# A kernel's opening on five queues: reordered, with a shorter statistics chain and more filler products

## The chip, the cores and the metric

The kernel runs on one core of a Trainium2 chip. The metric is the device time of one launch in microseconds (us). Engines are named as the profile names them: PE (TensorE products), PEld (its weight loads), DVE (VectorE), ACT (ScalarE), POOL (GpSimd) and SP (SyncE, which here issues most DMAs).

## The reference

Two layers on x of shape (2, 1024, 2048), with a context of (2, 2048, 2048).

```python
def fake_quant(x, scale, zp):
    q = jnp.clip(jnp.round(x / scale + zp), 0.0, 255.0)
    return (q - zp) * scale

# layer 1: the normalized x and the context are both quantized to bytes
x = x + jnp.matmul(fake_quant(_layernorm(x), s1, z1), fake_quant(ctx, s2, z2))

# layer 2: a base product with bias, and a two-of-eight mixture of rank-16 products
xf = _layernorm(x)
base = xf @ W_base.T + b_base
probs = jax.nn.softmax(xf @ W_router.T)          # top 2 kept, renormalized -> w
lora = einsum('ter,eor,te->to', einsum('td,erd->ter', xf, lora_A), lora_B, w) * 2.0
x = x + base + lora
```

`_layernorm` is (x - mean) / sqrt(var + 1e-5) over the last axis.

## The kernel before

**Tiles.** The rows of x are 16 row tiles T of 128 rows, eight for each half b of the batch. The first product is made for 32 column tiles n (16 for each b); each has three chunks c of 342 columns of rows. `chunk(n, c)` is 16 products, 128x128 by 128x342, into one of four PSUM banks in turn (`RING`); it needs its ring slot read by `take_y` four chunks earlier in `ORDER`, and the bytes of three, six or eight row tiles (`NEED`). The first three n run chunk by chunk across n: (0,0), (1,0), (2,0), (0,1) and so on; from n = 3 the three chunks of one n follow each other.

**A row tile's path.** DVE takes statistics of the 2048 elements in four instructions and aggregates them (`ln_stats_of`, lines 926 and 929), copies the mean and adds epsilon to the variance (936, 937). ACT takes the root (`ln_std_of`, 692). DVE makes scale and shift with a reciprocal and one Newton step (`ln_scale_of`, 944 to 955): seven small instructions, of which each but one waits for the one before. Some tiles go through this in pairs (`LN_GROUPS`: rows 0, 1, 2 alone, then 3+4, 5+6, 7 alone, then pairs). ACT makes the bytes (`ln_bytes_of`, 701), or for rows 4 and 6 POOL (`row_bytes_of`, 1628). PE turns the bytes (`turn`, 1669, eight transposes), ACT copies them out of PSUM as f16 (`ln_copy`, 709), and PE sums them (`row_sum`, 1677).

**A column tile's path.** SP loads 1 MB of context, POOL makes bytes (`ctx_bytes_of`, 1614), and ACT (`ctx_act_of`, 718, for n in `ON_ACT`) or DVE (`ctx_ready_of`, 988, the others) makes f16. DVE takes each chunk's result (`take_y`, 1003). When the third chunk of n is taken, ACT adds a column, writes the high part and squares (724, 732, 740), and DVE writes the low part and adds up the squares (`lo_of` 1009, `acc_of` 1022). `load_xt(n)` on SP waits for these of n - 3.

**The order around the change.** Each engine's queue is written out by hand. PE's opening is lines 1720 to 1748: row tiles 0 to 2, 16 filler products of ones (`keep_busy`, 1716, a result that nobody reads), then chunks (0,0) and (1,0), and after that turns, row sums and chunks mixed. DVE's opening is lines 1045 to 1153, ACT's 742 to 791, SP's 470 to 498. `LOAD_AT`, `STATS_AT`, `SCALE_AT`, `STD_AT` and `BYTES_AT` say at which n a row tile of the second half is loaded, measured, scaled and made into bytes. `rows[1]` has two slots, so row tile 11 loads only when the bytes of row tile 9 are made; POOL makes the bytes of rows 4 and 6 behind the context bytes of n = 2 and 3 (`POOL_AT`).

Of the kernel before, what the change touches and what calls it, by code (L numbers as in the profile page):

```python
# [8 lines left out]
ALU = mybir.AluOpType  # L9
# [3 lines left out]
P = 128  # L13
# [14 lines left out]
TT = TOKENS // P  # L28
# [29 lines left out]
POOL_AT = {2: 4, 3: 6}  # L58
LOAD_AT = {4: 11, 6: 12, 8: 13, 10: 14, 12: 15}
# [3 lines left out]
ON_ACT = list(range(2, STEPS, 2))  # L63
# [29 lines left out]
def xattn_ffn(nc, x, xT, ctx, s1, z1, s2, z2, w_t, w_n, bias, ar, b_t, outT):  # L93

    es = ExitStack()
    with es:
# [94 lines left out]
        lnt = [small(f"lnt{s}", [P, 8, 2]) for s in range(2)]  # L191
        par = small("par", [P, 25])
# [24 lines left out]
        def pc(i):  # L217
            return par[:, i:i + 1]
# [5 lines left out]
        T0, T1, T2, NIS1 = pc(21), pc(22), pc(23), pc(24)  # L224
# [12 lines left out]
        def sem(name):  # L237
            return es.enter_context(nc.semaphore(name))
# [38 lines left out]
        ln_shift = sem("ln_shift")  # L277
# [165 lines left out]
        def _(sp):  # L443
# [237 lines left out]
        def _(act):  # L681
# [6 lines left out]
            def ln_std_of(g):  # L688

                t0, w = LN_GROUPS[g]  # L690
                act.wait_ge(ln_var, g + 1)
                A.activation(std1[:, t0:t0 + w], lnt[g % 2][:, 0, 0:w], ACT.Sqrt).then_inc(ln_std, 1)
# [59 lines left out]
            ln_std_of(3)  # L752
            ln_bytes_of(3)
            ctx_act_of(2)
# [11 lines left out]
            ctx_act_of(4)  # L766

            for n in range(STEPS):
                col_add_of(n)
                if n == JT + 13:  # L770
                    act.wait_ge(ar_lo, 1)
                hi_of(n)
                if n in STD_AT:
                    ln_std_of(STD_AT[n])
                sq_of(n)
                if n == 0:
                    ln_copy(TT)
                if n == 1:
                    ln_bytes_of(TT + 1)
                if n + 3 in ON_ACT and n + 3 > 4:  # L780
                    ctx_act_of(n + 3)
                if n == 2:
                    ln_copy(TT + 1)
                if n in BYTES_AT:
                    ln_bytes_of(BYTES_AT[n])
                if n - 1 in BYTES_AT:
                    ln_copy(BYTES_AT[n - 1])
                if n == JT + 11:
                    act.wait_ge(ar_scaled, 1)
                    A.activation(ar_p[0][:, :, 0:AR], ar_f[:, :, :], ACT.Copy, scale=asc[:, 0:1]).then_inc(ar_hi, 1)  # L790
# [123 lines left out]
        def _(dve):  # L914
            V = nc.vector

            def ln_stats_of(T):
# [19 lines left out]
                V.tensor_scalar(lnt[g % 2][:, 0, 0:w], mv[g % 2][:, 0:w, 1], EPS, None, ALU.add).then_inc(ln_var, 1)  # L937

            def ln_scale_of(g):

                t0, w = LN_GROUPS[g]
                n = lnt[g % 2]
                dve.wait_ge(ln_std, g + 1)
                V.reciprocal(n[:, 1, 0:w], std1[:, t0:t0 + w]).then_inc(ln_newton, 1)
                dve.wait_ge(ln_newton, 4 * g + 1)
                V.scalar_tensor_tensor(n[:, 2, 0:w], n[:, 1, 0:w], -0.5, n[:, 1, 0:w], ALU.mult, ALU.mult).then_inc(ln_newton, 1)
                dve.wait_ge(ln_newton, 4 * g + 2)
                V.tensor_tensor(n[:, 2, 0:w], n[:, 2, 0:w], n[:, 0, 0:w], ALU.mult).then_inc(ln_newton, 1)
                dve.wait_ge(ln_newton, 4 * g + 3)
                V.scalar_tensor_tensor(n[:, 3, 0:w], n[:, 2, 0:w], 1.5, n[:, 1, 0:w], ALU.add, ALU.mult).then_inc(ln_newton, 1)  # L950
                dve.wait_ge(ln_newton, 4 * g + 4)
                V.tensor_scalar(n[:, 4, 0:w], n[:, 3, 0:w], IS1, None, ALU.mult)
                V.scalar_tensor_tensor(n[:, 6, 0:w], n[:, 3, 0:w], NIS1, mv[g % 2][:, 0:w, 0], ALU.mult, ALU.mult).then_inc(ln_shift, 1)
                dve.wait_ge(ln_shift, g + 1)
                V.tensor_scalar(n[:, 5, 0:w], n[:, 6, 0:w], Z1, None, ALU.add).then_inc(ln_scale, 1)
# [67 lines left out]

            V.memset(onesF[:, :], 1.0)
# [12 lines left out]
            ins.then_inc(ln_stat, 1)  # L1037
            dve.wait_ge(par_turned, 1)
# [6 lines left out]
            ln_stats_of(0)  # L1045
            dve.wait_ge(par_step, 1)
            V.tensor_scalar(NIS1, IS1, -1.0, None, ALU.mult)
# [16 lines left out]
            ctx_ready_of(1)  # L1064
# [32 lines left out]
            bound(0)  # L1097

# [551 lines left out]
        def _(pe):  # L1650
# [301 lines left out]
```

## Time and profile before

| | us |
|---|---|
| median of 3 runs | 1002.93 (1002.04 to 1003.18) |
| the profiled execution's own time | 1003.91 |
| its span, first to last instruction | 1002.1 |
| mean granted TensorE clock | 0.991 of full |

The profile's page gives busy time by engine, the chain of work that ended last, and the costliest groups. The timeline gives instructions of one engine in order of time, merged where the same line repeats; the idle time in front of each stands in square brackets, with what ended it. The windows give each engine's busy time in a stretch, with the granted clock (1.00 is 2.4 GHz, 0.50 is 1.2 GHz). After about 95 us the kernel is the rest of the first product, then the router and rank-16 products, and from about 345 us the large base products.

### The profile page before, as it was taken

Reading aid. Unit: us, or ns where it says so; the run is one execution under the profiler, and the core shown is the slowest. Engines: PE = TensorE matmul, PEld = TensorE weight load, DVE = VectorE, ACT = ScalarE, POOL = GpSimd, SP = SyncE. Lnnn points to the kernel's source line nnn. Section 1 sums busy time; section 2 is a strip of 40 time slices with the busy share of each in tenths; the row PEclk is TensorE's granted clock in tenths of the full one; section 3 lists DMA queues with packets and bytes.
Section 4 is the critical chain, followed back from the end, with each engine's and each line's share of the span. In section 5 each row is a group of like instructions: output and inputs, shape, how many; then the busy total and the mean of one; then the engine's idle time right before and its main releaser. Section 6 shows DMA issues by size and latency. Waiting matters only on the chain.

```text
span 1002.1 us, 14914 instructions
## 1 busy us (share of the span) xinstructions
PE 964.9 (96%) x5765; PEld 523.2 (52%) x5765; DVE 794.9 (79%) x1457; ACT 430.5 (43%) x467; POOL 136.7 (14%) x176
## 2 busy tenths in 40 slices
PE   1798999999999999999999999999999999999998
PEld 1565666666689644444444444444444444444444
DVE  7977877989746677997887777857789788798885
ACT  4667879565643335545443344212222223322310
POOL 3615335456200000000000000000000000000000
PEclk9799999999999999999999999999999999999999
DMA  9837767788542517876765564248544143242220
GB/s 372 362 106 300 263 278 286 250 302 299 202 161 74 153 51 220 249 271 188 227 226 201 174 217 149 79 155 291 185 142 136 59 152 116 79 137 91 98 74 32
DMA packets 62311, 185.65 MB, mean 185 GB/s; under 512 B 6896, under 2 KB 19488, under 8 KB 56096
## 3 DMA queue, kind: packets, MB, share of 16 engines
q1 hardware_dynamic: 58648, 174.18, 48.7%
q0 software_dynamic: 1280, 2.12, 2.4%
q10 hardware_dynamic: 2312, 8.39, 2.1%
q8 instruction: 46, 0.75, 0.3%
q14 instruction: 25, 0.20, 0.1%
HBM read 151.07 MB, written 33.60 MB: 184 GB/s over the span
## 4 chain that ended last, share of the span: by engine, by line
PE 85%; DVE 0%; issue 0%
PE pair L1846 33%; PE pair L1870 28%; PE pair L1689 13%; PE pair L1808 5%; PE pair L1818 4%; PE pair L1882 1%; PE pair L1697 0%; PE pair L1788 0%; PE pair L1669 0%; PE pair L1709 0%; DVE sq L1541 0%; DVE u L1543 0%; PE pair L1703 0%; PE pair L1795 0%; PE pair L1782 0%; PE pair L1713 0%
## 5 line engine op out<-in xcount | busy, mean ns | idle before, releaser
L1846 PE MATMUL pair<-x2p,w_p 128*128 128x512 f16 x1536 | 337.0, 379 | 0.0
L1846 PEld LDWEIGHTS pair<-x2p,w_p 128*128 128x128 f16 x1536 | 150.2, 98 | 180.5
L1689 PE MATMUL pair<-q1T,ctx_q 128*128 128x342 f16 x1536 | 232.6, 313 | 6.3 <-DVE xt L1003 6.3
L1689 PEld LDWEIGHTS pair<-q1T,ctx_q 128*128 128x128 f16 x1536 | 149.6, 98 | 84.7 <-issue 8.2
L1870 PE MATMUL pair<-x2p,w_slot 128*128 128x512 f16 x744 | 163.8, 379 | 0.0
L827 ACT ACTIVATE sq<-pair,lsc 128x512 f32<-128x512 f32 x64 | 43.5, 681 | 212.2 <-PE pair L1818 176.4
L1614 POOL TENSOR_SCALAR ctx_u<-ctx_f,par 128x512 uint8<-128x512 f32 x128 | 112.0, 889 | 142.1 <-DMA ctx_f<-in_ctx 104.0
L1870 PEld LDWEIGHTS pair<-x2p,w_slot 128*128 128x128 f16 x744 | 72.7, 98 | 87.9
L855 ACT ACTIVATE w_slot<-w_q,usc 128x1024 f16<-128x1024 f32 x32 | 36.5, 1146 | 89.8 <-DVE usc L1447 27.2
L1870 PE MATMUL pair<-x2p,x2p 128*128 128x512 f16 x336 | 74.3, 379 | 0.0
L724 ACT ACTIVATE xt<-xt,colt 128x1024 f32<-128x1024 f32 x32 | 36.7, 1146 | 53.9 <-DVE xt L1003 53.9
L1009 DVE SCALAR_TENSOR_TENSOR x2p<-xt,xs,x2p 128x1024 f16<-128x1024 f32 x32 | 42.3, 1322 | 21.1 <-ACT x2p L732 20.9
L1471 DVE SCALAR_TENSOR_TENSOR w_slot<-w_q,usc,w_slot 128x1024 f16<-128x1024 f32 x32 | 40.6, 1282 | 22.8 <-ACT w_slot L855 22.8
L811 ACT ACTIVATE w_p<-w_f,wsc 128x1024 f16<-128x1024 f32 x32 | 34.9, 1138 | 50.1 <-DVE wsc L1216 50.1
L855 ACT ACTIVATE x2p<-w_q,usc 128x1024 f16<-128x1024 f32 x24 | 27.4, 1146 | 65.6 <-DVE usc L1447 15.8
L1003 DVE SCALAR_TENSOR_TENSOR xt<-pair,par,xt 128x342 f32<-128x342 f32 (+1 forms) x96 | 53.5, 564 | 2.5 <-PE pair L1689 2.3
L1870 PEld LDWEIGHTS pair<-x2p,x2p 128*128 128x128 f16 x336 | 32.9, 98 | 39.6
L1870 PE MATMUL pair<-x2p 128*128 128x512 f16 x240 | 52.9, 379 | 0.0
L1818 PE MATMUL pair<-hwT,b_p 128*128 128x512 f16 x192 | 51.7, 379 | 0.0
L1416 DVE SCALAR_TENSOR_TENSOR u<-sq,bias_s,u 128x512 f32<-128x512 f32 x63 | 47.4, 752 | 2.2
L1808 PE MATMUL pair<-ar_p,x2p 128*128 128x137 f16 x768 | 48.3, 224 | 0.0
L1808 PEld LDWEIGHTS pair<-ar_p,x2p 128*128 128x128 f16 x768 | 48.1, 98 | 0.1
(223 smaller groups left out, 1068.0 us busy)
## 6 DMA issues: line engine op xcount, KB each, us to landing
ctx_f<-in_ctx SPq DMA_DIRECT2D x32, 1024.0 KB, 7.6
xt<-in_xT SPq DMA_DIRECT2D x32, 512.0 KB, 4.5
w_r<-in_w_n SPq DMA_DIRECT2D x32, 512.0 KB, 6.9
w_f<-in_w_t SPq DMA_DIRECT2D x32, 512.0 KB, 5.6
w_q<-in_w_t SPq DMA_DIRECT2D x32, 512.0 KB, 5.1
outT<-u SPq DMA_DIRECT2D x63, 256.0 KB, 3.2
rows<-in_x SPq DMA_DIRECT2D x15, 1024.0 KB, 9.4
x_kept<-xt ACTq DMA_DIRECT2D x16, 512.0 KB, 4.3
```

Source lines behind the costliest of these rows:

```text
L827: A.activation(sq[m % 2][:, :], lora_bank(m)[:, :], ACT.Copy, scale=by).then_inc(lora_taken, 1)
L855: A.activation(w_of(i, p, 0), w_q[s][:, :, :], ACT.Copy, scale=usc[:, i % 2, (3 if by == 4 else 2):(4 if by == 4 else 3)]).then_inc(s_hi, 1)
L1003: V.scalar_tensor_tensor(xt[n % 3][:, t], bank[at % RING][:, 0:WIDTH[c]], S12, xt[n % 3][:, t], ALU.mult, ALU.add).then_inc(y_taken, 1)
L1009: V.scalar_tensor_tensor(x2p[b][:, j, 1, :], xt[n % 3][:, :], xs[:, b, 0:1], x2p[b][:, j, 0, :], ALU.mult, ALU.subtract).then_inc(lo_done, 1)
L1416: V.scalar_tensor_tensor(o[:, :], s[:, :], bias_s[:, j:j + 1], o[:, :], ALU.add, ALU.add).then_inc(u_ready, 1)
L1471: V.scalar_tensor_tensor(w_of(i, p, 1), w_q[s][:, :, :], usc[:, i % 2, (3 if by == 4 else 2):(4 if by == 4 else 3)], w_of(i, p, 0), ALU.mu ...
L1614: ins = G.tensor_scalar(ctx_u[n % 2][:, c], ctx_f[n % 2][:, c], IS2, Z2, ALU.mult, ALU.add)
L1689: ins = M.matmul(bank[at % RING][:, 0:W3], ctx_q[n % NQ][:, k, :], q1T[b][:, k, c * W3:(c + 1) * W3], start=(k == 0), stop=(k == KT - 1))
L1808: ins = M.matmul(h_tile(b, t), x2p[b][:, k, xh, t * P:(t + 1) * P], ar_p[ah][:, k, :], start=(k == 0 and q == 0), stop=(k == KT - 1 and q ...
L1818: ins = M.matmul(lora_bank(m)[:, :], b_p[s][bh][:, :], hwT[b][hh][:, t], start=(q == 0), stop=(q == 2))
L1846: M.matmul(base_bank(m)[:, :], w_p[j % 2][wh][:, k, :], x2p[0][:, k, xh, t], start=(k == 0 and q == 0), stop=(k == KT - 1 and q == 2))
L1870: ins = M.matmul(product_bank(i, p)[:, :], w_of(i, p, wh)[:, k // 4, (k % 4) * P:(k % 4 + 1) * P], x_of(p, k, xh), start=(k == 0 and q == ...
```

## The change

- `ln_stats_of` negates the mean as a third small instruction. `ln_std_of` reads the variance itself, with epsilon as the activation's bias, and waits for the aggregation in place of the epsilon sum. `ln_scale_of` now has dependent steps reciprocal, product (with the scaled reciprocal beside it), a*(-0.5)+1.5, product, shift; the two steps with a per-row scalar operand are issued once for each tile of a pair.
- DVE aggregates row 0 before the parameters; `ctx_ready_of(1)` goes to ACT and `ctx_act_of(2)` to DVE; the statistics of row 9 move ahead of the parameter block, and `ln_scale_of(6)` (rows 8 and 9) ahead of `take_y(0, 1)` and its successor.
- ACT makes row 9's bytes before the loop over n; the context tile 4 and the copy of row 8 each move accordingly.
- POOL makes the bytes of rows 4 and 6 one context tile earlier.
- SP issues row tile 11's load before `load_xt(3)`; it was at n = 4.
- PE: 48 more filler products (16 become 64) in three places; `chunk(1, 0)` moves behind `turn(4)`, `chunk(1, 1)` behind `row_sum(6)`, `row_sum(3)` ahead of `chunk(2, 0)`.

```diff
-POOL_AT = {2: 4, 3: 6}
-LOAD_AT = {4: 11, 6: 12, 8: 13, 10: 14, 12: 15}
+POOL_AT = {1: 4, 2: 6}
+LOAD_AT = {6: 12, 8: 13, 10: 14, 12: 15}
-ON_ACT = list(range(2, STEPS, 2))
+ON_ACT = [1] + list(range(4, STEPS, 2))
...
             load_rows(TT + 2)
+            load_rows(TT + 3)
             for n in range(3, STEPS):
                 load_xt(n)
...
-                act.wait_ge(ln_var, g + 1)
-                A.activation(std1[:, t0:t0 + w], lnt[g % 2][:, 0, 0:w], ACT.Sqrt).then_inc(ln_std, 1)
+                act.wait_ge(ln_stat, 2 * (t0 + w))
+                A.activation(std1[:, t0:t0 + w], mv[g % 2][:, 0:w, 1], ACT.Sqrt, bias=eps[:, :]).then_inc(ln_std, 1)
...
             ln_std_of(3)
+            ctx_act_of(1)
             ln_bytes_of(3)
-            ctx_act_of(2)
...
             ln_bytes_of(TT)
-            ctx_act_of(4)
+            ln_bytes_of(TT + 1)
...
                 if n == 0:
+                    ctx_act_of(4)
+                if n == 1:
                     ln_copy(TT)
-                if n == 1:
-                    ln_bytes_of(TT + 1)
...
                 V.reciprocal(n[:, 1, 0:w], std1[:, t0:t0 + w]).then_inc(ln_newton, 1)
+                dve.wait_ge(ln_var, g + 1)
                 dve.wait_ge(ln_newton, 4 * g + 1)
-                V.scalar_tensor_tensor(n[:, 2, 0:w], n[:, 1, 0:w], -0.5, n[:, 1, 0:w], ALU.mult, ALU.mult).then_inc(ln_newton, 1)
+                for m in range(w):
+                    V.scalar_tensor_tensor(n[:, 2, m:m + 1], n[:, 1, m:m + 1], n[:, 0, m:m + 1], n[:, 1, m:m + 1], ALU.mult, ALU.mult)
+                V.tensor_scalar(n[:, 3, 0:w], n[:, 1, 0:w], IS1, None, ALU.mult).then_inc(ln_newton, 1)
                 dve.wait_ge(ln_newton, 4 * g + 2)
-                V.tensor_tensor(n[:, 2, 0:w], n[:, 2, 0:w], n[:, 0, 0:w], ALU.mult).then_inc(ln_newton, 1)
+                V.tensor_scalar(n[:, 2, 0:w], n[:, 2, 0:w], -0.5, 1.5, ALU.mult, ALU.add).then_inc(ln_newton, 1)
                 dve.wait_ge(ln_newton, 4 * g + 3)
-                V.scalar_tensor_tensor(n[:, 3, 0:w], n[:, 2, 0:w], 1.5, n[:, 1, 0:w], ALU.add, ALU.mult).then_inc(ln_newton, 1)
+                V.tensor_tensor(n[:, 4, 0:w], n[:, 2, 0:w], n[:, 3, 0:w], ALU.mult).then_inc(ln_newton, 1)
                 dve.wait_ge(ln_newton, 4 * g + 4)
-                V.tensor_scalar(n[:, 4, 0:w], n[:, 3, 0:w], IS1, None, ALU.mult)
-                V.scalar_tensor_tensor(n[:, 6, 0:w], n[:, 3, 0:w], NIS1, mv[g % 2][:, 0:w, 0], ALU.mult, ALU.mult).then_inc(ln_shift, 1)
-                dve.wait_ge(ln_shift, g + 1)
-                V.tensor_scalar(n[:, 5, 0:w], n[:, 6, 0:w], Z1, None, ALU.add).then_inc(ln_scale, 1)
+                for m in range(w):
+                    ins = V.scalar_tensor_tensor(n[:, 5, m:m + 1], n[:, 4, m:m + 1], n[:, 6, m:m + 1], Z1, ALU.mult, ALU.add)
+                ins.then_inc(ln_scale, 1)
...
             ln_stats_of(4)
-            ctx_ready_of(1)
             ln_scale_of(3)
...
             ln_scale_of(4)
+            ctx_ready_of(2)
+            ln_stats_of(7)
             take_y(1, 0)
-            ln_stats_of(7)
...
             ln_stats_of(TT)
+            ln_stats_of(TT + 1)
...
             bound(0)
+            ln_scale_of(6)
...
             chunk(0, 0)
-            chunk(1, 0)
+            keep_busy(24)
             turn(3)
             row_sum(2)
             turn(4)
+            chunk(1, 0)
+            row_sum(3)
+            keep_busy(8)
             chunk(2, 0)
-            row_sum(3)
             turn(5)
             row_sum(4)
             turn(6)
+            keep_busy(16)
             row_sum(5)
             chunk(0, 1)
-            chunk(1, 1)
             turn(7)
             row_sum(6)
+            chunk(1, 1)
             chunk(2, 1)
```

## Rows read from the trace of the kernel before

**Rows 1.** The page, part 1: busy time of each engine.

```profile
PE 964.9 (96%) x5765; PEld 523.2 (52%) x5765; DVE 794.9 (79%) x1457; ACT 430.5 (43%) x467; POOL 136.7 (14%) x176
```

**Rows 2.** Windows: stretch, length, busy time of each engine, granted clock, DMA share, GB/s.

```profile
26.00:47.00 21.00, 15.64 (x156) 11.17 (x153) 19.74 (x53) 14.15 (x11) 13.56 (x17) 0.82 1.01 411
47.00:66.05 19.05, 19.05 (x162) 12.66 (x163) 13.85 (x53) 10.47 (x7) 5.24 (x8) 0.84 0.18 60
94.40:250.00 155.60, 153.48 (x1112) 103.23 (x1110) 133.02 (x211) 111.42 (x89) 73.88 (x85) 1.00 0.77 285
```

**Rows 3.** Waits of PE, whole span: total us, times, longest.

```profile
PE pair L1669 <- ACT q1u L701: 18.5, 6, 5.3
PE pair L1689 <- DVE xt L1003: 6.3, 5, 3.2
```

**Rows 4.** PE timeline: start, length, line, tiles, count, idle before and releaser.

```profile
26.13 1.87 PE L1718 MATMUL pair<-ones 128*128 128x128 f16 x16
28.02 5.45 PE L1689 MATMUL pair<-q1T,ctx_q 128*128 128x342 f16 x32
...
35.47 0.62 PE L1669 MATMUL pair<-ident,q1w 128*128 128x128 f16 x8 [2.00 <-ACT q1u L701]
...
47.43 7.65 PE L1689 MATMUL pair<-q1T,ctx_q 128*128 128x342 f16 x32
54.92 0.61 PE L1669 MATMUL pair<-ident,q1w 128*128 128x128 f16 x8
55.36 0.54 PE L1677 MATMUL pair<-ones,q1T 128*128 128x1 f16 x16
...
87.81 6.26 PE L1689 MATMUL pair<-q1T,ctx_q 128*128 128x342 f16 x32 [3.16 <-DVE xt L1003]
94.36 14.11 PE L1689 MATMUL pair<-q1T,ctx_q 128*128 128x342 f16 x96
```

**Rows 5.** Windows: the stretch at the low clock.

```profile
44.00:53.00 9.00, 7.85 (x66) 4.98 (x64) 8.04 (x40) 5.90 (x4) 3.47 (x5) 0.50 0.33 135
```

**Rows 6.** DVE timeline: chains of row 1 (POOL busy) and row 7 (POOL idle).

```profile
14.99 0.16 DVE L944 RECIPROCAL lnt<-std 128x1 f32<-128x1 f32 x1 [0.33 <-ACT std L692]
...
17.36 0.21 DVE L955 TENSOR_SCALAR lnt<-lnt,par 128x1 f32<-128x1 f32 x1
...
41.73 2.46 DVE L926 BATCH_NORM_STATS2 stats<-rows 128x6 f32<-128x512 f32 x4
44.22 0.26 DVE L929 BATCH_NORM_AGGREGATE mv<-stats 128x2 f32<-128x24 f32 x1
...
45.10 0.17 DVE L944 RECIPROCAL lnt<-std 128x1 f32<-128x1 f32 x1 [0.27 <-ACT std L692]
...
46.26 0.21 DVE L955 TENSOR_SCALAR lnt<-lnt,par 128x1 f32<-128x1 f32 x1
```

**Rows 7.** ACT timeline: bytes of rows 3 and 5, a copy, first column add.

```profile
33.32 2.10 ACT L701 ACTIVATE q1u<-rows,lnt 128x2048 uint8<-128x2048 f32 x1 [3.93 <-DVE lnt L955]
...
41.37 2.10 ACT L701 ACTIVATE q1u<-rows,lnt 128x2048 uint8<-128x2048 f32 x1 [0.21 <-DVE lnt L955]
...
44.97 1.95 ACT L709 ACTIVATE q1T<-pair,par 128x2048 f16<-128x2048 uint8 x1
...
65.41 1.13 ACT L724 ACTIVATE xt<-xt,colt 128x1024 f32<-128x1024 f32 x1
```

**Rows 8.** POOL timeline: context tile 1, bytes of row 6.

```profile
21.63 4.02 POOL L1614 TENSOR_SCALAR ctx_u<-ctx_f,par 128x512 uint8<-128x512 f32 x4 [4.32 <-DMA ctx_f<-in_ctx]
...
41.43 3.02 POOL L1628 TENSOR_SCALAR q1u<-rows,lnt 128x512 uint8<-128x512 f32 x4 [0.95 <-DVE lnt L955]
```

**Rows 9.** SP timeline: the load of row tile 11.

```profile
75.71 0.33 SPq L454 DMA_DIRECT2D rows<-in_x  x1
```

**Rows 10.** DVE timeline: statistics of row tile 11, and the take behind it.

```profile
84.08 2.47 DVE L926 BATCH_NORM_STATS2 stats<-rows 128x6 f32<-128x512 f32 x4 [2.64 <-DMA rows<-in_x]
...
87.10 0.57 DVE L1003 SCALAR_TENSOR_TENSOR xt<-pair,par,xt 128x342 f32<-128x342 f32 x1
```

More of the change, by code:

```diff
@@ L190, in xattn_ffn @@
         std1 = small("std1", [P, BATCH * TT])
-        lnt = [small(f"lnt{s}", [P, 8, 2]) for s in range(2)]
-        par = small("par", [P, 25])
+        lnt = [small(f"lnt{s}", [P, 7, 2]) for s in range(2)]
+        eps = small("eps", [P, 1])
+        par = small("par", [P, 24])
         asum = small("asum", [P, AR])
@@ L223, in xattn_ffn @@
         S12, ND1S, ND2S, DDS, YB = pc(16), pc(17), pc(18), pc(19), pc(20)
-        T0, T1, T2, NIS1 = pc(21), pc(22), pc(23), pc(24)
+        T0, T1, T2 = pc(21), pc(22), pc(23)
         xs = small("xs", [P, 2, 2])
@@ L276, in xattn_ffn @@
         stat_ready = sem("stat_ready")
-        ln_shift = sem("ln_shift")
         fold_step = sem("fold_step")
@@ L936, in ln_stats_of @@
                 V.tensor_copy(mean1[:, t0:t0 + w], mv[g % 2][:, 0:w, 0])
-                V.tensor_scalar(lnt[g % 2][:, 0, 0:w], mv[g % 2][:, 0:w, 1], EPS, None, ALU.add).then_inc(ln_var, 1)
+                V.tensor_scalar(lnt[g % 2][:, 0, 0:w], mv[g % 2][:, 0:w, 1], EPS, None, ALU.add)
+                V.tensor_scalar(lnt[g % 2][:, 6, 0:w], mv[g % 2][:, 0:w, 0], -1.0, None, ALU.mult).then_inc(ln_var, 1)
             def ln_scale_of(g):
@@ L1022, in acc_of @@
                     V.tensor_tensor(acc[:, :], acc[:, :], pair[2][:, :], ALU.add).then_inc(acc_done, 1)
+            V.memset(eps[:, :], EPS)
             V.memset(onesF[:, :], 1.0)
@@ L1037, in _ @@
             ins.then_inc(ln_stat, 1)
+            ln_stats_of(0)
             dve.wait_ge(par_turned, 1)
@@ L1044, in _ @@
             V.tensor_scalar(C2, Z2, ROUND, ROUND, ALU.add, ALU.subtract).then_inc(par_step, 1)
-            ln_stats_of(0)
             dve.wait_ge(par_step, 1)
-            V.tensor_scalar(NIS1, IS1, -1.0, None, ALU.mult)
             V.tensor_scalar(C1, C1, 0.0, 255.0, ALU.max, ALU.min)
@@ L1137, in ar_low @@
                                        ar_p[0][:, :, 0:AR], ALU.mult, ALU.subtract).then_inc(ar_lo, 1)
-            ln_stats_of(TT + 1)
             take_y(0, 1)
-            ln_scale_of(6)
             take_y(1, 1)
```

## Prediction, before the changed kernel was run

> **What bounds the kernel now.** I read the page's busy times first: PE is busy 96% of the span [rows 1], so a gain can only come from where PE idles or runs at its low clock. The windows by stretch say where that is. From 26 to 47 us PE is busy 15.6 of 21 us at a clock of 0.82; from 47 to 66 it is full but at 0.84; from 94.4 to 250 it idles 2.1 us in 155.6 at full clock [rows 2]. PE's waits name the causes: 18.5 us in all for a row tile's bytes, six times, and 6.3 us for DVE to free a ring slot, once for 3.2 [rows 3]. In PE's timeline these are the idle times in front of turns in the opening (2.0 us before row 3's turn at 35.47) and the 3.16 us before 87.81 [rows 4]. Behind a wait the clock is low: 0.50 all through 44 to 53 us [rows 5], where two chunks take 7.65 us; six chunks at full clock take 14.11, that is 2.35 each, so the two lost 2.95 [rows 4].
>
> **One landmark carries the sum:** chunk (6,0), which starts at 94.36 [rows 4]. Everything behind it is bound by PE [rows 2], so what it moves, the end moves.
>
> **PE's floor up to the landmark.** From the start of chunk (0,0) PE must do 18 chunks, 18 x 2.35 = 42.3 us, eight turns and six row sums. A turn followed by a row sum takes from 54.92 to 55.90 [rows 4], 0.98, of which the next instruction covers about a tenth: about 0.9 a pair, so 0.45 each and 14 x 0.45 = 6.3. With the bound's transpose 49 us. Before, it took 94.36 - 28.02 = 66.3 us, so 17 us are lost to idling and clock: that is all there is to win there.
>
> **The added products.** Sixteen took 1.87 us, 0.117 each [rows 4]. The change adds 24 + 8 + 16 = 48: 5.6 us of PE time. They cost nothing only where PE would idle. Their worth is the clock that they keep up, not time of their own. The floor becomes 49 + 5.6 = 54.6, and since the first chunks ran slow at the start (two took 5.45, not 4.70 [rows 4], which I expect again) 55.4 us.
>
> **The shorter chain.** On a quiet POOL the chain of one row ran from the reciprocal at 45.10 to 46.47, 1.37 us, and the aggregation's start to the reciprocal took 0.88 [rows 6]. Six dependent steps become five after the reciprocal's input: about 0.20 less, and the last two of the old steps each read a parameter operand at slightly more, so about 0.3 in all. The root no longer waits for the copy and the epsilon sum, another 0.3. The negated mean is one more independent instruction, about 0.07, under ACT's root. So 0.6 a row alone; for a pair two more instructions take 0.15 back. With POOL at work the same chain took 14.99 to 17.57, 2.58 us [rows 6]: 1.2 more, since about every second dependent step was held. I price that at three holds before and two after, so row 1 gains about 1.0.
>
> The Trainium skill, "GPSIMD Engine Reference", section "Key points", says that GpSimd shares its SBUF interfaces with VectorE, and that VectorE instructions in a two-port mode or with two SBUF inputs contend. This case's rows agree, 2.58 us against 1.37 for the same seven instructions. By the skill's "VectorE: DVE Perf Modes", section "Rules for kernel authors", it is the number of operations that should be kept small, not the semaphores; the change keeps seven to nine small instructions for one row and adds two for a pair, so by that page the chain part brings nothing. That result is the third rival below.
>
> **The opening, walked.** I moved each engine's order forward with the durations of the trace: statistics 2.46 + 0.26, bytes 2.10 on ACT and 3.02 on POOL, copy 1.95 [rows 6 to 8].
> - Row 1's bytes start at about 16.7 on ACT and row 2's at 21.8; copy (2) ends at about 27 and chunk (0,0) starts at 27.2 (28.02 before), the 16 old products being in front of it.
> - DVE has no context tile 1 between statistics and scale: rows 3 and 4 are scaled by 29.2, and ACT, which makes context tile 1 under that (until 29.8), starts row 3's bytes at 29.7, not 33.32 [rows 7]. POOL makes row 4's until 32.3, ahead of context tile 2 (landed at 29.4, so it is delayed to 35.3). DVE then makes tile 2 after scale(4), ready at about 38.0.
> - Rows 5 and 6 are scaled by 36.7: ACT's bytes at 37.1, not 41.37 [rows 7]; POOL's until 40.7, not 44.45 [rows 8], with 1 us for DVE's context tile beside it, as in the 4.02 for 3.02 of [rows 8].
> - PE then runs with hardly a gap: chunk (0,0) and 24 products to 33.3, turn 3, row sum, turn 4, chunk (1,0) to 37.0, row sum, 8 products to 38.3, chunk (2,0) to 40.7, turns 5 and 6 and 16 products to 43.9, row sum, chunk (0,1) to 46.7, turn 7, 0.6 us idle for copy (6) at 47.7, chunks (1,1) and (2,1) to 52.8. The 24 products end 1.5 us after row 3's bytes (31.8) and the 16 end 0.9 after copy (5): about 2 us of them lie on PE's path.
> - DVE does the statistics of rows 8 and 9 and the parameters by 52.7 and scale(6) by 54; take (0,1) waits for it until 54.5, and chunk (1,2), which needs that ring slot, begins at 55.8: covered. If the products were not there, this DVE order would be what is late.
> - Chunk (2,2) ends at 61.0, against 66.0 before, the end of a stretch in [rows 2].
>
> **The stall at 87.8.** Row tile 11's load was issued at 75.71 [rows 9], DVE waited 2.64 us for it and PE's ring stood until the take at 87.10 [rows 10]. Now SP issues it as soon as row 9's bytes are made. ACT makes those ahead of its loop, until about 58.1, behind scale(6); the first column add then starts at 58.1, not 65.41 [rows 7]: 7.3 earlier. Queued behind the new SP wait are `load_xt(3)` and context tile 6; they need column tile 0's low part (about 61.7) anyway, so the wait is covered by 3.6 us. Context tile 4 sits in ACT's loop in place of row 9's bytes (1.9 for 2.1), so the loop keeps its pace. The take of (4,0) comes at 87.10 - 2.64 - 7.3 = 77.2; by the longer walk 78.0. PE, at 61.0 + seven chunks + a turn, is there at 77.9. So the stall goes and what is late next is take (4,1), at 81.1, which PE wants at 80.4: 0.7 us. The landmark comes at 83.9, PE's floor alone at 27.2 + 55.4 = 82.6. Its clock was also low after 87.81 (6.26 us for two chunks [rows 4], 1.6 more than 4.70); this is in the difference.
>
> **The sum.** 94.36 - 83.9 = 10.5 us by the walk, 11.8 by the floor. The walk has DVE and ACT at most 1 us behind PE in several places, and places the context conversions beside POOL at their short times; I take 1 us off for that: 9.5. Everything after the landmark is as before; the 2.1 us idle there [rows 2] I leave. The profiled execution, 1003.91, would become 994.4; it lies 1.0 above the median of the runs, so against the median: 1002.93 - 9.5 = 993.4. The other moves (row 0 before the parameters 0.2 us, epsilon's memset) are in the walk.
>
> **Rivals.**
> 1. *The clock falls once or twice in spite of the products.* For it: between 33 and 43 us only two chunks run, among turns and row sums, and before the clock fell twice in that stretch (0.82 over the stretch [rows 2]). Against: the idle times in front of it were 2 us and are now under 1. Price: up to 2.95 us for two chunks [rows 4], of which the ring's slack returns a third: 2 to 4 us, 995.5 to 997.5.
> 2. *DVE becomes the bound.* It is busy 19.7 of 21 us between 26 and 47 [rows 2] and gets more instructions. Each row's chain held by POOL as in [rows 6] costs 1.2; three such beyond the walk make 3.5 us late at the landmark: 997.
> 3. *The chain brings nothing, only the moves do* (the page's rule on counts): rows 1, 2 and 7 alone and the two pairs each give back 0.3 to 1.0, together 2 us on the path: 995.5.
> 4. *The early load does not end the stall*: something else of tile 4 (its slot, xt) is late as well. Then 3.16 + 1.6 come back: 998.2.
> 5. *Slower.* The 48 products lie wholly on the path because PE, not the bytes, is what the opening waits for, and the row chain wins nothing: +5.6, 1008.5. It decides from the point where bytes and clock give back less than 5.6 us; the idle times of 2 us in front of row 3's turn [rows 4] and the 18.5 in all [rows 3] speak against it.
>
> **How the numbers follow.** Forecast (with its own range 991.5 to 995.0) 0.52; clock 0.20; DVE 0.10; chain 0.07; stall stays 0.05; slower 0.03; a return of the gain later, to about no change, 0.03. The range is 991.3 (floor reached, less 0.2 of spread) to 998.0: it takes in the first three rivals. Faster by over 0.2% (2 us, about what a measurement can tell here) 0.94, within 0.03, slower 0.03.
>
> **What would show it.** Chunk (6,0) near 84 us. Row 3's bytes on ACT at 29.7 and row 5's at 37. No PE idle over 1 us between 27 and 84. Granted clock 1.00 in 44 to 53. Row 11's load issued near 58 and no DMA wait ahead of its statistics. The chain of a row alone near 1.05 us with POOL idle. Wrong would be: a clock of 0.50 anywhere between 35 and 60, a new wait of SP or ACT near 58, or the wait for a ring slot returning near 80 at over 1 us.

## The result, and the profile after

The changed kernel takes 993.15 us (median of 4 runs, 992.48 to 994.51), the kernel before 1002.48 us (4 runs, 999.76 to 1003.18). The ratio is 0.9914, with a 95% interval of 0.9892 to 0.9936: 8.6 us, or 6.4 to 10.8, are gone. A second measurement at a later time gave 0.9915 (0.9895 to 0.9935). The prediction on record was 993.4 us, 9.5 us less than before.

The profiled execution of the changed kernel took 994.51 us, with a span of 992.7 against 1002.1. Busy times, from the page's part 1 (this answers [rows 1]):

```profile
PE 961.9 (97%) x5813; PEld 523.3 (53%) x5813; DVE 793.7 (80%) x1469; ACT 431.2 (43%) x467; POOL 139.4 (14%) x176
```

PE has 48 more instructions, which take 3.2 us, and yet is busy 3.0 us less. So the other matmuls are busy 6.2 us less: those that ran at half clock before take their full-clock time now. PE's idle time is 6.4 us less, of which the added products fill 3.2. The same stretches as in [rows 2], and that of [rows 5]:

```profile
26.00:47.00 21.00, 18.14 (x212) 13.27 (x211) 19.90 (x57) 15.57 (x12) 13.47 (x17) 0.92 0.98 391
47.00:66.00 19.00, 18.50 (x165) 12.86 (x163) 16.62 (x60) 15.02 (x12) 6.53 (x8) 1.00 0.50 177
94.40:250.00 155.60, 155.10 (x1124) 104.66 (x1122) 136.00 (x222) 110.41 (x90) 76.65 (x84) 1.00 0.77 281
44.00:53.00 9.00, 8.19 (x93) 5.79 (x91) 8.49 (x36) 6.68 (x5) 3.15 (x5) 1.00 0.40 141
```

From 44 to 53 us the granted clock is 1.00 where it was 0.50. Behind 94.4 us PE idles 0.5 us in place of 2.1. PE's waits over the span (to be held against [rows 3]):

```profile
PE pair L1674 <- ACT q1u L702: 13.6, 3, 6.0
PE pair L1694 <- DVE ctx_q L993: 2.4, 1, 2.4
PE pair L1854 <- DVE w_p L1236: 1.7, 1, 1.7
PE pair L1694 <- DVE xt L1008: 1.6, 2, 1.1
PE pair L1682 <- ACT q1T L710: 0.8, 2, 0.5
```

The wait for a row tile's bytes is down from six times to three, which are rows 0, 1 and 2, all ahead of chunk (0,0). Of the 18.5 us before, these three had 14.0. So only 4.5 us were there to be won, and the 18.5 that the prediction holds against its rival 5 overstates it. The wait for a ring slot is down from 6.3 to 1.6 us. Two new ones stand beside them: 2.4 us for context tile 2, and 1.7 us for a base weight near 392 us. PE's timeline of the opening, as in [rows 4]:

```profile
26.87 2.95 PE L1694 MATMUL pair<-q1T,ctx_q 128*128 128x342 f16 x16
29.65 1.50 PE L1723 MATMUL pair<-ones 128*128 128x128 f16 x24
31.23 0.62 PE L1674 MATMUL pair<-ident,q1w 128*128 128x128 f16 x8
...
38.31 4.04 PE L1694 MATMUL pair<-q1T,ctx_q 128*128 128x342 f16 x16 [2.45 <-DVE ctx_q L993]
...
45.28 2.48 PE L1694 MATMUL pair<-q1T,ctx_q 128*128 128x342 f16 x16
...
71.43 9.67 PE L1694 MATMUL pair<-q1T,ctx_q 128*128 128x342 f16 x64
82.20 2.49 PE L1694 MATMUL pair<-q1T,ctx_q 128*128 128x342 f16 x16 [1.11 <-DVE xt L1008]
...
84.97 14.11 PE L1694 MATMUL pair<-q1T,ctx_q 128*128 128x342 f16 x96
```

The landmark, chunk (6,0), starts at 84.97 us, not at 94.36 [rows 4]: 9.39 us earlier, which is the 9.4 us of the spans. The stall of 3.16 us is gone. Behind the landmark the two executions take the same 907.7 us; there the changed one wins back 1.6 us of ring waits and loses 1.7 at the weight. That this part is equal is partly luck. A second profile of the changed kernel took 909.3 us behind its landmark, and over all fourteen profiled executions below this part goes from 905.0 to 910.3 us.

Some 1 us of the 9.39 is not the change's either. The profiled execution of the kernel before started chunk (0,0) at 28.02 us. Two altered kernels below, whose edits act only behind that point (the early load alone and the products alone), started it at 26.93 and 27.11, as early as the changed kernel (26.87). From chunk (0,0) to the landmark PE took 66.3 us before and 58.1 after, 8.2 us less. The ratio, 8.6 us, rests on all runs and is the number to go by. DVE's lines for row tile 11, against [rows 10]:

```profile
74.44 2.46 DVE L927 BATCH_NORM_STATS2 stats<-rows 128x6 f32<-128x512 f32 x4
...
77.90 0.56 DVE L1008 SCALAR_TENSOR_TENSOR xt<-pair,par,xt 128x342 f32<-128x342 f32 x1
```

The statistics find their rows there, and the take of (4,0) comes at 77.90, 9.20 us earlier than at 87.10.

### The profile page after: what moved, and what is told of

Same layout as the page of the kernel before. It is cut to its first block, busy times and chain, and to the rows that moved or that the text cites. A ratio compares the mean times of both kernels' runs of the same rounds, so it can differ in the third digit from the quotient of the medians.

```text
span 992.7 us, 15032 instructions
## 1 busy us (share of the span) xinstructions
PE 961.9 (97%) x5813; PEld 523.3 (53%) x5813; DVE 793.7 (80%) x1469; ACT 431.2 (43%) x467; POOL 139.4 (14%) x176
## 3 DMA queue, kind: packets, MB, share of 16 engines
q0 software_dynamic: 1280, 2.12, 2.1%
## 4 chain that ended last, share of the span: by engine, by line
PE 79%; DVE 4%; DMA 3%; issue 0%; ACT 0%; DVEq 0%
PE pair L1878 29%; PE pair L1854 27%; PE pair L1694 13%; PE pair L1816 5%; PE pair L1826 4%; DMA scratch<-w_max 1%; DMA spread<-scratch 1%; DVE w_p L1236 1%; PE pair L1890 1%; PE pair L1702 0%; ACT w_p L812 0%; DVE cent L1292 0%; DVE cent L1331 0%; DVE u L1401 0%; DVE u L1421 0%
## 5 line engine op out<-in xcount | busy, mean ns | idle before, releaser
L1694 PE MATMUL pair<-q1T,ctx_q 128*128 128x342 f16 x1536 | 228.5, 309 | 4.1 <-DVE ctx_q L993 2.4
L1646 POOL DMA_DIRECT2D scratch<-w_max x16 | 8.9, 554 | 282.2 <-DVE w_max L1210 263.7
```

The source lines that it names most:

```text
L1694: ins = M.matmul(bank[at % RING][:, 0:W3], ctx_q[n % NQ][:, k, :], q1T[b][:, k, c * W3:(c + 1) * W3], start=(k == 0), stop=(k == KT - 1))
```

## The experiments

Twelve more measurements were made, of eleven kernels (the changed one and ten altered ones), four at a time on one chip. Each is compared with the kernel before on the same chip. "Landmark" is the start of chunk (6,0) in the one execution that was profiled; ratios rest on all runs. One part alone, added to the kernel before:

| kernel | ratio (95%) | us by ratio | landmark |
|---|---|---|---|
| early load alone | 0.9979 (0.9964 to 0.9993) | -2.1 | 89.31 |
| 48 products alone | 0.9978 (0.9965 to 0.9991) | -2.2 | 92.35 |
| moves alone | 0.9962 (0.9951 to 0.9973) | -3.8 | 87.30 |
| shorter chain alone | 0.9991 (0.9974 to 1.0008) | -0.9, not resolved | 91.15 |
| all four, the change | 0.9914 and 0.9915 | -8.6 | 84.97 and 84.77 |

The first and the third row both make row 9's bytes early on ACT, so they overlap by that much.

One part taken out of the change, or one thing altered in it:

| kernel | ratio (95%) | landmark |
|---|---|---|
| without the 48 products | 0.9946 (0.9922 to 0.9971) | 84.75 |
| with the late load | 0.9951 (0.9931 to 0.9971) | 89.14 |
| with the old chain | 0.9920 (0.9894 to 0.9946) | 85.40 |
| 46 products ahead of chunk (2,0) | 0.9919, 0.9923 | 84.50, 85.75 |
| context tile 2 ahead of scale(4) | 0.9906 (0.9888 to 0.9924) | 84.01 |
| 46 products, and row 11's statistics later | 0.9947 (0.9931 to 0.9964) | 83.4 |

### Without the added products

```diff
             chunk(0, 0)
-            keep_busy(24)
             turn(3)
...
-            keep_busy(8)
             chunk(2, 0)
...
             turn(6)
-            keep_busy(16)
             row_sum(5)
```

> The changed kernel without its 48 added products; the 16 old ones stay. My theory: in the changed kernel's trace the 48 took about 3.2 us and lay mostly in front of waits, so what they buy is the clock. Without them PE idles longer in front of the turns of rows 3 and 5 and the clock falls earlier: chunk (6,0) starts 0.5 to 3 us later than its 84.97 us in the changed kernel. Rival (they only cost): it starts up to 2 us earlier and no stretch at 0.50 is longer than the one there now.

PE's timeline of the profiled execution:

```profile
31.40 0.62 PE L1674 MATMUL pair<-ident,q1w 128*128 128x128 f16 x8 [2.12 <-ACT q1u L702]
...
38.50 2.50 PE L1694 MATMUL pair<-q1T,ctx_q 128*128 128x342 f16 x16 [2.93 <-DVE ctx_q L993]
...
124.77 4.81 PE L1694 MATMUL pair<-q1T,ctx_q 128*128 128x342 f16 x32 [1.21 <-DVE xt L1008]
```

The windows of the same execution:

```profile
26.00:47.00 21.00, 14.61 (x176) 10.46 (x173) 19.90 (x57) 15.95 (x12) 13.55 (x17) 1.00 0.97 383
```

DVE's timeline of the same execution, statistics of row tiles 13 and 14:

```profile
104.37 2.47 DVE L927 BATCH_NORM_STATS2 stats<-rows 128x6 f32<-128x512 f32 x4 [1.17 <-DMA rows<-in_x]
...
121.43 2.47 DVE L927 BATCH_NORM_STATS2 stats<-rows 128x6 f32<-128x512 f32 x4 [2.54 <-DMA rows<-in_x]
```

Both idle times are longer than 2 us, yet the clock did not fall in this execution, and the landmark came as early as with the products. So by this one execution the rival is right. The ten runs say something else: their median is 996.58 us, their spread 994.62 to 1000.38, and their mean clock from 0.995 to 1.000, where the changed kernel's was 0.998 to 1.000 in four runs and 0.996 to 1.000 in six more. The products are worth 3.2 us by the two ratios (0.9946 less 0.9914), though the intervals of the two leave about as much uncertainty. On this chip the median is 2.3 to 2.5 us above those of the two kernels that keep products (994.27 and 994.07 us, below), and when added alone they gave 2.2 us (0.9 to 3.5).

Whether an idle time of 2 us costs the clock differs from execution to execution. That the products pay by keeping the clock up is shown only in part. The three runs at a mean clock of 1.000 took 996.36, 996.81 and 997.65 us here. The changed kernel's four such runs took 992.48 to 993.55, and the three with the old chain, on the same chip as here, 992.14 to 994.07. So the clock is not the whole of it. In this profiled execution the loss lies behind the landmark, at full clock: 910.3 us against 907.7. PE waits there four times for a ring slot, 3.4 us (0.5 in the changed kernel). Ahead of these waits DVE stands idle for row tiles 13, 14 and 15 to land (1.17, 2.54 and 2.58 us; in the changed kernel 1.60 and 1.29 for the last two alone). That is the wait of the stall at 87.8 again, for later row tiles, whose place in SP's order the change left as it was. Why it is longer without the products, no run shows.

### With the late load

```diff
-LOAD_AT = {6: 12, 8: 13, 10: 14, 12: 15}
+LOAD_AT = {4: 11, 6: 12, 8: 13, 10: 14, 12: 15}
...
             load_rows(TT + 2)
-            load_rows(TT + 3)
```

> The changed kernel with row tile 11's load back at n = 4, everything else as changed. My theory, from the walk: the load is then issued about 6 to 8 us later (SP stands behind load_xt(4)), DVE waits for it, and the ring stall comes back in part: chunk (6,0) 1 to 4 us after 84.97. Rival (the earlier bytes of row 9 alone did it, since SP reaches n = 4 early enough): within 0.5 us of 84.97.

```profile
70.13 7.13 PE L1693 MATMUL pair<-q1T,ctx_q 128*128 128x342 f16 x48
81.54 7.32 PE L1693 MATMUL pair<-q1T,ctx_q 128*128 128x342 f16 x32 [4.28 <-DVE xt L1007]
...
89.14 11.06 PE L1693 MATMUL pair<-q1T,ctx_q 128*128 128x342 f16 x75
```

SP's issue of row tile 11's load, and DVE's statistics of it:

```profile
68.43 0.43 SPq L454 DMA_DIRECT2D rows<-in_x  x1
...
77.74 2.47 DVE L926 BATCH_NORM_STATS2 stats<-rows 128x6 f32<-128x512 f32 x4 [3.96 <-DMA rows<-in_x]
```

In PE's timeline the stall is back, longer than before (4.28 us), and with it the low clock: two chunks in 7.32 us where 4.81 is usual. The landmark moves by 4.17 us, and the ratio by 3.7 us. My theory's 1 to 4 was a little short. The load is issued at 68.43 us; in the changed kernel it is the second of two row loads issued from 56.72 to 59.03. DVE then waits 3.96 us for it. Row 9's bytes are as early here as in the changed kernel, so SP's own order is part of the cause, not only those bytes.

### With the old chain

```diff
-                act.wait_ge(ln_stat, 2 * (t0 + w))
-                A.activation(std1[:, t0:t0 + w], mv[g % 2][:, 0:w, 1], ACT.Sqrt, bias=eps[:, :]).then_inc(ln_std, 1)
+                act.wait_ge(ln_var, g + 1)
+                A.activation(std1[:, t0:t0 + w], lnt[g % 2][:, 0, 0:w], ACT.Sqrt).then_inc(ln_std, 1)
...
 # and ln_stats_of and ln_scale_of as in the kernel before
```

> The changed kernel with the old statistics chain (epsilon sum ahead of the root, Newton step of seven instructions); all moves, the early load and the products stay. My theory: each scaled group is 0.3 to 1.0 us later, rows 0 to 6 make five groups, so row 3's bytes start 1.5 to 2.5 us after their 29.09 and chunk (6,0) starts 1 to 3 us after 84.97. Rival (the number of instructions counts, not the dependent steps): within 0.5 us.

The landmark is at 85.40, 0.43 us late, and the ratio 0.9920 against 0.9914 is no difference that can be told. Row 3's bytes start at 30.23 us, 1.14 after their 29.09 and not the 1.5 to 2.5 of my theory. So the rival's number came out, but not for its reason: the row bytes are later, but the clock did not fall at chunk (2,0), which took 2.50 us and not 4.04. Against the first profile with 46 products below, whose clock stayed up there too, the landmark is 0.9 us late. DVE's timeline of this kernel, then of the changed one, for row 2 with POOL idle:

```profile
19.13 0.26 DVE L930 BATCH_NORM_AGGREGATE mv<-stats 128x2 f32<-128x24 f32 x1
...
19.98 0.16 DVE L945 RECIPROCAL lnt<-std 128x1 f32<-128x1 f32 x1 [0.27 <-ACT std L693]
...
21.14 0.21 DVE L956 TENSOR_SCALAR lnt<-lnt,par 128x1 f32<-128x1 f32 x1
```

```profile
18.58 0.26 DVE L930 BATCH_NORM_AGGREGATE mv<-stats 128x2 f32<-128x24 f32 x1
...
19.21 0.16 DVE L947 RECIPROCAL lnt<-std 128x1 f32<-128x1 f32 x1
19.48 0.22 DVE L951 SCALAR_TENSOR_TENSOR lnt<-lnt 128x1 f32<-128x1 f32 x1
19.61 0.21 DVE L952 TENSOR_SCALAR lnt<-lnt,par 128x1 f32<-128x1 f32 x1
...
20.24 0.22 DVE L959 SCALAR_TENSOR_TENSOR lnt<-lnt,par 128x1 f32<-128x1 f32 x1
```

The shorter chain wins something in itself. From the aggregation to the reciprocal it is 0.63 us, not 0.85. From the reciprocal to the shift's end it is 1.25, not 1.37: the step with a per-row scalar that the reciprocal feeds starts 0.27 us after it, where the old one started after 0.20. So a row alone wins 0.34 us. For the pair of rows 3 and 4 the new steps took 27.32 to 28.87, 1.55 us, the old ones 28.46 to 29.87, 1.41: the last part is longer by 0.14.

### 46 products ahead of chunk (2,0), twice

```diff
-            keep_busy(8)
+            keep_busy(46)
             chunk(2, 0)
```

> The changed kernel with 46 products in place of 8 ahead of chunk (2,0), where PE idled 2.45 us and the chunk then took 4.04 us at half clock. 38 more at 0.0625 us are 2.4 us. My theory: they fill the idle time, the clock stays at 1.00 there, chunk (2,0) takes 2.5 us and the landmark chunk (6,0) comes up to 1.5 us earlier than 84.97, less what DVE's order allows. Rival (DVE and ACT set the landmark, PE has slack): the clock stays up but the landmark is within 0.4 us.

```profile
35.66 2.73 PE L1723 MATMUL pair<-ones 128*128 128x128 f16 x46
38.42 2.50 PE L1694 MATMUL pair<-q1T,ctx_q 128*128 128x342 f16 x16
...
81.73 2.48 PE L1694 MATMUL pair<-q1T,ctx_q 128*128 128x342 f16 x16 [0.65 <-DVE xt L1008]
```

The idle time is filled and the chunk runs at full clock, but PE then waits 0.45 us for take (4,0) and 0.65 us for take (4,1), and the landmark is at 84.50. That is the rival, though 0.47 us is just past its 0.4. The second run:

> The changed kernel with 46 products ahead of chunk (2,0), a second time, now beside the changed kernel. My theory after its first run (clock 0.999 or 1.00 in all runs, landmark 84.50, median 994.27): the clock is steady but the earlier landmark is given back to DVE's ring waits behind it, so the median is within 0.7 us of the changed kernel's. Rival (the steady clock pays): 1 to 2 us below it.

The clock was 0.999 or 1.00 in every run of both (8 and 5), and the landmark of the second 85.75. By the ratios, 0.9923 against 0.9915 for the changed kernel on the same chip, nothing is gained. The median, 995.02 us, is 1.84 above the changed kernel's, outside my 0.7 on the bad side. A steady clock in this place frees time that PE only waits away later. Nor do 46 products make it certain: in the variant of this kernel further down two chunks at 47.70 us took 6.48 us, not 4.81.

### Early load alone

```diff
-LOAD_AT = {4: 11, 6: 12, 8: 13, 10: 14, 12: 15}
+LOAD_AT = {6: 12, 8: 13, 10: 14, 12: 15}
...
+            load_rows(TT + 3)
...
             ln_bytes_of(TT)
+            ln_bytes_of(TT + 1)
             ctx_act_of(4)
...
-                if n == 1:
-                    ln_bytes_of(TT + 1)
```

> The kernel before with one part of the change: row tile 11's load right behind row tile 10's, and row 9's bytes right behind row 8's on ACT (all else old, the old PE order, chain and products). My theory: the DVE wait of 2.64 us and PE's ring stall of 3.16 us before 87.81 go, with the clock drop behind it; chunk (6,0) comes 3 to 5 us before its 94.36 of the kernel before. Rival (the take of (4,0) is late for another reason, since ACT now makes row 9's bytes ahead of the first column add): less than 1.5 us.

```profile
77.81 4.81 PE L1689 MATMUL pair<-q1T,ctx_q 128*128 128x342 f16 x32 [0.76 <-DVE xt L1003]
83.57 2.48 PE L1689 MATMUL pair<-q1T,ctx_q 128*128 128x342 f16 x16 [0.96 <-DVE xt L1003]
86.55 2.48 PE L1689 MATMUL pair<-q1T,ctx_q 128*128 128x342 f16 x16 [0.49 <-DVE xt L1003]
...
89.31 14.10 PE L1689 MATMUL pair<-q1T,ctx_q 128*128 128x342 f16 x96
```

The stall of 3.16 us is gone with the low clock behind it; waits of 0.5 to 1.0 us stand in its place. The landmark is 5.05 us earlier; 1.34 of them this execution had already at chunk (0,1), which starts at 46.09 here and at 47.43 in [rows 4], before the edit acts. The runs show only 2.1 us. In the profile four later ring waits sum to 2.9 us (2.1 before), and a wait of 1.2 us for the base weight is there.

### Products alone

> The kernel before with the 48 products alone, in the waits in front of the turns of rows 3 and 5 and of row sum 5, its old order kept. My theory: with the row chain as late as before they keep the clock up, PE's low stretches between 36 and 53 us shrink, chunk (2,2) ends 1 to 3 us earlier, but DVE's order and the ring stall stay, so chunk (6,0) moves by under 1 us: the stall at 85 to 88 us takes it back. Rival (clock is what the opening loses): chunk (6,0) 2 us or more earlier.

The edit is the 24, 8 and 16 products at the corresponding places of the old order. Chunks (0,1) and (1,1) took 4.81 us, not 7.65, and chunk (2,2) started at 59.53, not 63.69. But PE then stood longer for the take of (4,0):

```profile
84.93 7.13 PE L1689 MATMUL pair<-q1T,ctx_q 128*128 128x342 f16 x32 [4.44 <-DVE xt L1003]
```

At the landmark 2.0 us of 4.2 were left (92.35), and 0.9 of these the execution had already at chunk (0,0), before the edit acts. That is more than the "under 1" I wrote, and just the rival's bound; the direction, that the stall takes half of it back, is as expected.

### Moves alone

> The changed kernel without the early load, without the 48 products and with the old chain: only the orders of DVE, ACT, POOL and PE. My theory, by difference (chain 0.4 us and load 4 us in the runs before this one): chunk (6,0) at 88 to 91 us, so 3.5 to 6 us of the 9.4 are the moves. Rival (the parts only work together): within 2 us of 94.36.

The landmark is at 87.30, better than my 88 to 91, and the moves are the largest part, 3.8 us by ratio. No run splits them, so which of the moves on DVE, ACT, POOL and PE pay is open. Even the stall is only 2.39 us here: SP issues row tile 11's load at 69.28 us, not at 75.71 [rows 9], still at n = 4 but in a loop that starts earlier.

### Chain alone

> The kernel before with the shorter chain alone (epsilon as the root's bias, five dependent steps). By the prediction's sizes five groups win 0.3 to 1.0 us each, in all 2 us. What the run with the old chain in the changed kernel showed is 0.4 us at chunk (6,0). My theory now: row 3's bytes start 1 to 2.5 us earlier than 33.32, but PE's order and DVE's context tile 1 keep chunk (0,1) from following: chunk (6,0) 0 to 1.5 us earlier than 94.36, median within 1 us of before. Rival (in the old order the chain is the critical path): 2 to 4 us.

Row 3's bytes start at 31.35 on ACT (33.32 in [rows 7]), 2.0 us earlier, as expected. The landmark is at 91.15, 3.2 us earlier, outside what I had written; the ratio, 0.9991 with an interval across one, is what I had written. The two fit if the execution of [rows 4] was a slow draw: its clock was 0.991, and 26 other runs of the kernel before had 0.989 to 0.998. The clock here was 0.995. Two chunks from 46.38 took 6.12 us, not 7.65, and the clock did not fall behind the ring stall, which was as long as before (3.18 us). I take the runs.

### Context tile 2 first

```diff
-            ln_scale_of(4)
-            ctx_ready_of(2)
+            ctx_ready_of(2)
+            ln_scale_of(4)
```

> The changed kernel with DVE's context tile 2 ahead of scale(4). PE idled 2.45 us for that tile, which POOL had ready at 34.98 us and DVE made at 36.97 behind take (0,0) and scale(4). My theory: chunk (2,0) starts 1.3 to 1.7 us earlier and the clock drop at 38 to 41 us goes, but the bytes of rows 5 and 6 come 1.3 us later, so chunk (0,1) starts within 0.7 us of where the changed kernel's does when its clock stays up (43.8 us) and chunk (6,0) within 0.5 us of 84.7. Rival (the idle time is the opening's bound): chunk (6,0) 1 us or more earlier.

```profile
35.90 2.50 PE L1694 MATMUL pair<-q1T,ctx_q 128*128 128x342 f16 x16 [0.99 <-DVE ctx_q L993]
...
42.62 2.48 PE L1694 MATMUL pair<-q1T,ctx_q 128*128 128x342 f16 x16
...
81.24 2.49 PE L1694 MATMUL pair<-q1T,ctx_q 128*128 128x342 f16 x16 [1.48 <-DVE xt L1008]
84.01 14.10 PE L1694 MATMUL pair<-q1T,ctx_q 128*128 128x342 f16 x96
```

Chunk (2,0) is 2.4 us earlier, chunk (0,1) 2.7 (45.28 in the changed kernel), and the landmark 1.0. Most of the other 1.7 us is given back in small waits: for a copy on ACT (1.14 us, not 0.50), for the bound on DVE (0.29), for take (4,0) (0.21) and for take (4,1) (1.48, not 1.11). This execution's opening ran about 1.0 us ahead already at row 3's turn (30.27 against 31.23), before the edit acts, so little of the 1.0 is the edit's. The ratio, 0.9906 against 0.9915 on the same chip, doesn't tell it from the changed kernel.

### Row 11's statistics later

```diff
-STATS_AT = {3: 11, 6: 12, 7: 13, 9: 14, 11: 15}
-SCALE_AT = {4: 7, 8: 8, 12: 9}
-STD_AT = {3: 7, 7: 8, 11: 9}
-BYTES_AT = {3: 10, 5: 11, 7: 12, 9: 13, 11: 14, 13: 15}
+STATS_AT = {4: 11, 6: 12, 7: 13, 9: 14, 11: 15}
+SCALE_AT = {5: 7, 8: 8, 12: 9}
+STD_AT = {4: 7, 7: 8, 11: 9}
+BYTES_AT = {4: 10, 5: 11, 7: 12, 9: 13, 11: 14, 13: 15}
```

> The changed kernel with 46 products ahead of chunk (2,0), and row 11's statistics, its root and scale and row 10's bytes one column tile later (n = 4, 4, 5, 4). In the changed kernel and three variants PE waits 0.6 to 1.1 us each for take (3,2) or (4,1), behind that DVE block. My theory: those waits go and chunk (6,0) comes at 83.4 to 84.2 instead of 84.97. Rival (DVE's total is what counts; the block only moves its wait): within 0.4 us of 84.50, or the waits between 110 and 152 us grow by as much and the median is within 0.5 us of the changed kernel's.

PE's timeline:

```profile
71.68 16.43 PE L1694 MATMUL pair<-q1T,ctx_q 128*128 128x342 f16 x112
88.51 2.49 PE L1694 MATMUL pair<-q1T,ctx_q 128*128 128x342 f16 x16 [0.40 <-DVE xt L1008]
...
99.35 0.61 PE L1674 MATMUL pair<-ident,q1w 128*128 128x128 f16 x8 [0.94 <-ACT q1T L710]
```

DVE's timeline, statistics of row tile 14:

```profile
122.52 2.47 DVE L927 BATCH_NORM_STATS2 stats<-rows 128x6 f32<-128x512 f32 x4 [2.15 <-DMA rows<-in_x]
```

Seven chunks run without a wait from 71.68, so chunk (6,0), the sixth of them, starts at 71.68 + 5 x 2.35 = 83.4. 0.45 us of this lead is row 10's turn, which now stands behind chunk (6,2). Then waits appear at 88, 99, 109, 112, 125 and 143 us, 3.9 us in all, and the median is 996.65 us, 3.3 us worse than the changed kernel by the ratios. The waits (for takes (4,0) and (4,1), not (3,2) as I had written) went, as in my theory, and came back behind the landmark, as in the rival, but its "within 0.5 us" is far off. Its reason is not shown either. DVE is not simply full there: it idles 0.67, 2.15 and 1.43 us for row tiles 13, 14 and 15. An early landmark alone says little.

### The changed kernel again

> The changed kernel itself, beside the other three of this call on the same chip. My theory: median 992.5 to 994.5 us, chunk (6,0) at 84.5 to 85.5 us, its mean granted clock 0.997 or more in every run, where the kernel before spread from 0.989 to 0.998. Rival (the first result was a lucky draw of the clock): median above 995.

993.18 us and a landmark of 84.77 are as expected; the clock was 0.996 in one of the six runs, against my 0.997 for all. No variant beats it by more than the measurement tells.

## Why the prediction was right

**The time.** 993.4 against 993.15 us, and 9.5 us of gain against 8.6 (6.4 to 10.8). The mechanism held: PE's idle times and low clock in the opening went, and the stall with them. That the number came so close is partly luck, through terms that cancel, as told below. The method, one landmark behind which all is bound by PE, held for this pair of executions (9.39 us at the landmark, 9.4 in the spans). It is good to some 2 or 3 us and no better, since PE still waits up to 4.2 us behind the landmark, for ring slots and a weight, and that differs between executions of one kernel.

**The walk.** Row 3's bytes were forecast at 29.7 and started at 29.09; row 5's at 37.1 and 37.09; the first column add at 58.1 and 58.59; the take of (4,0) at 78.0 and 77.90; the landmark at 83.9 by the walk, 84.97 in fact. The 1 us taken off for DVE's and ACT's lateness was used up, mostly by chunk (2,0) at half clock rather than by that lateness: chunk (0,1) already started 0.9 us later than walked. Take (4,1), named as "what is late next" with 0.7 us, was: PE waited 1.11 us for it, and between 0.64 and 1.48 us in its second execution and in the five variants that kept the early load and row 11's place.

**The signs of being wrong.** Two of the three listed ones came true: a clock of 0.50 between 35 and 60 (38.3 to about 41.5 us), and a wait for a ring slot near 80 of over 1 us (1.11). "No PE idle over 1 us" failed with them, and a row's chain alone took 1.25 us, not 1.05. The time held in spite of them.

**The stall.** Right in place and size. Its term was 3.16 + 1.6; with the late load back, the stretch from chunk (4,1) to the landmark took 19.01 us (70.13 to 89.14), in the changed kernel 13.54: 5.5 us, of it 4.28 idle and 2.5 at the slow clock, less the waits that stand there otherwise. That I had at 4.8.

**The products were mis-sized.** I took 0.117 us for one, from the 16 ahead of the first chunk [rows 4]. These take 1.87 us in the changed kernel again, but the 24 behind the first chunk took 1.50 us, 0.0625 each, and the 48 took 1.50 + 0.61 + 1.06 = 3.2, not 5.6. That the first 16 run at the low rate of a PE that has hardly worked is my reading of it (chunk (0,0) behind them took 2.95 us, not 2.48); the clock column reads 1.00 there. So PE reached chunk (2,0) at 35.9, not at 38.3, and there idled 2.45 us for context tile 2, which I had at 38.0 and which came at 38.25. The two errors cancel at that point. The clock then fell (rival 1), and chunk (2,0) took 4.04 us: 1.6 us, which I had not in the walk. Behind it the ring's slack returned most: the first profile with 46 products shows 0.47 us at the landmark, the second none.

**The chain was mis-sized.** 0.34 us for a row alone, not 0.6; a pair gets 0.24 on its way to the reciprocal and gives back 0.14. Under POOL row 1's chain took 14.71 to 16.17, 1.46 us in place of 2.58 [rows 6], 1.1 against the 1.0 forecast, but that is luck: POOL began its context tile only at 15.14 us there, behind the chain's first steps. With POOL at work from the start the new chain took 2.01 us (the run of the chain alone) and the old one 2.39 (the run with the old chain), so about 0.4 to 0.6. In the time it is not to be told from nothing: 0.9991 alone, 0.6 us when taken out. Rival 3 was right that the chain brings next to nothing, and wrong that the sum would then be 2 us short.

By "VectorE: DVE Perf Modes" of the Trainium skill, "Rules for kernel authors", the count of instructions decides. The rows bear it out in part. On a quiet POOL a dependent instruction started about 0.18 to 0.27 us after its producer and an independent one 0.06 to 0.14 us after the one before it. So one dependent step less for a row paid a little, and the two more instructions for a pair cost more than that, 0.14 us net.

The Trainium skill's "GPSIMD Engine Reference", "Key points", says that GpSimd and VectorE share SBUF interfaces. The hold beside POOL was the larger price in this case: 2.58 us in place of 1.37 for the same seven instructions [rows 6].

**The parts.** Alone they sum to 2.1 + 2.2 + 3.8 + 0.9 = 9.0 us against 8.6 together. The agreement proves little: each interval is 1 to 2 us wide to either side, and row 9's early bytes are counted twice. At the landmarks they sum to 17.3 against 9.4. Each of the four is held against the one slow execution of the kernel before, and the parts overlap, since ring waits take back what is early.

**What stays open.** PE's wait for a base weight near 392 us (0.8 to 2.2 us) is in both profiles of the changed kernel and in six of the eleven profiles of altered kernels, and not in that of the kernel before. DVE waited 4.47 us for a bound that goes through memory at 382.67 us, shortly before, and 2.63 us in the kernel before; that this is the cause is not shown, since no run was made for it. Nor was one made with row tiles 13, 14 and 15 loaded earlier, though DVE's waits for them (1.60 and 1.29 us in the changed kernel) are what is left of ring waits behind the landmark.

## What to carry to other kernels

Find one instruction behind which one engine bounds nearly everything, walk each engine's order up to it by the durations of the trace, and take a rate only from a stretch that ran at the clock it will run at. Removing a wait pays only as far as the next engine's chain allows: two edits that removed or shortened PE's idle time ahead of chunk (2,0) (three profiles) moved the landmark by -1.0 to +0.8 us and the ratio by nothing that can be told. When a late load has caused one stall, look for the same wait at the loads behind it. Judge such parts by the medians of many runs: one profiled execution can be 3 us off at the landmark, and behind it the part that hardly any edit touched varied by 5 us.

## What the runs showed of the hardware

An idle time of PE between 2 and 3 us did or did not cost the clock. In the run without the products 2.12 and 2.93 us of idling left it at 1.00; in the changed kernel 2.45 us brought it to 0.50 for about 3 us. The 26 runs of the kernel before on one chip had mean clocks of 0.989 to 0.998 and times of 998.62 to 1007.5 us. DVE's small instructions are held by POOL's work in steps: in the changed kernel the last step of row 7's chain took 0.71 us in place of 0.22, with POOL at work on a context tile. POOL's four instructions there, 0.75 us each, end at about 42.64, 43.39 and 44.14 us, and that is when the chain's three held steps ended too (the first of them began at 42.00 and took 0.64):

```profile
42.99 0.40 DVE L956 TENSOR_TENSOR lnt<-lnt 128x1 f32<-128x1 f32 x1
43.43 0.71 DVE L959 SCALAR_TENSOR_TENSOR lnt<-lnt,par 128x1 f32<-128x1 f32 x1
```

```profile
41.13 3.01 POOL L1619 TENSOR_SCALAR ctx_u<-ctx_f,par 128x512 uint8<-128x512 f32 x4
```
